# Edge counts of a graph layer built for 10 destinations a step in place of 25

## The reference

```python
def _sage_layer(h, edge_src, edge_dst, deg_inv, W_self, W_neigh, b):
    msg = h[edge_src]
    agg = jax.ops.segment_sum(msg, edge_dst, num_segments=h.shape[0])
    mean = agg * deg_inv[:, None]
    return h @ W_self + mean @ W_neigh + b
...
deg_inv = 1.0 / jnp.maximum(deg, 1.0)
h = jax.nn.relu(_sage_layer(x, edge_src, edge_dst, deg_inv, W_self0, W_neigh0, b0))
out = _sage_layer(h, edge_src, edge_dst, deg_inv, W_self1, W_neigh1, b1)
...
x = x + gnn(layernorm(x), src, dst)     # 1250 nodes, width 1024, 40000 edges sorted by dst
x = x + ffn(layernorm(x))               # router, top 2 of 8 experts
```

## Time and profile before

| | us |
|---|---|
| median of 3 runs | 1111.09 |
| the 3 runs | 1113.34, 1111.09, 1102.71 |
| span of the profiled execution, first to last instruction | 1107.6 |
| busy PE, DVE, ACT, POOL in it | 1068.1, 618.0, 427.1, 193.4 |
| tiles 1 to 7 with the counts | about 63.3 to 309 |

### The profile page before, as it was taken

The page is one execution under the profiler, slowest core; times in us unless marked ns, Lnnn a source line. Parts: engine busy times, 40 slices in busy tenths (PEclk is TensorE's granted clock), DMA queues, the critical chain, the costliest instruction groups (busy, mean ns, idle before and its releaser), DMA issues.

```text
span 1107.6 us, 18245 instructions
## 1 busy us (share of the span) xinstructions
PE 1068.1 (96%) x6565; PEld 1015.3 (92%) x6565; DVE 618.0 (56%) x1090; ACT 427.1 (39%) x934; POOL 193.4 (17%) x192
## 2 busy tenths in 40 slices
PE   5999999999999999999999999999999989999995
PEld 4999999999999999999999999999999679999994
DVE  6678888888752344334323523273222467878883
ACT  5555434453311222121121112164322257777672
POOL 5500000000000002000200020002442124555532
PEclk9999999999999999999999999999999979999998
DMA  6332133213227560004201430276565187999971
GB/s 191 95 105 71 44 108 108 70 43 105 71 71 242 148 186 16 1 19 150 67 1 54 129 76 1 58 244 189 158 186 190 38 302 233 318 304 291 304 220 29
DMA packets 72794, 144.97 MB, mean 131 GB/s; under 512 B 12822, under 2 KB 51667, under 8 KB 68209
## 3 DMA queue, kind: packets, MB, share of 16 engines
q1 hardware_dynamic: 61041, 112.50, 31.7%
q0 software_dynamic: 10976, 30.74, 10.7%
q10 hardware_dynamic: 672, 0.32, 0.1%
HBM read 108.40 MB, written 42.96 MB: 137 GB/s over the span
## 4 chain that ended last, share of the span: by engine, by line
PE 91%; DVE 3%; issue 2%; DMA 1%; DVEq 1%; ACT 1%; POOLq 0%; SPq 0%; POOL 0%; ACTq 0%
PE ps L1482 20%; PE ps L976 14%; PE ps L1554 10%; PE ps L2132 9%; PE ps L1521 9%; PE ps L1211 8%; PE ps L2153 6%; PE ps L821 4%; PE ps L735 3%; PE ps L2118 2%; PE ps L716 1%; DVE key_hot L814 1%; PE ps L921 1%; PE ps L1540 1%; DVE adj L828 1%
## 5 line engine op out<-in xcount | busy, mean ns | idle before, releaser
L1444 POOL TENSOR_TENSOR s_rows<-s_rows,b1t 125x1368 f32<-125x1368 f32 (+3 forms) x9 | 23.7, 2655 | 572.1 <-DMA s_rows<-in_x 572.1
L828 DVE TENSOR_TENSOR adj<-ps,adj 125x250 f32 x212 | 87.7, 414 | 42.0 <-PE ps L821 33.7
L976 PE MATMUL ps<-h_lo,w_hi 128*128 128x418 f32 x336 | 108.6, 372 | 0.0
L976 PE MATMUL ps<-h_hi,w_hi 128*128 128x418 f32 x336 | 100.3, 379 | 0.0
L1521 PE MATMUL ps<-z_hi,adj 125*125 125x342 f32 (+1 forms) x300 | 95.0, 322 | 1.4 <-DVE s_rows L1753 1.4
L1521 PE MATMUL ps<-z_lo,adj 125*125 125x342 f32 (+1 forms) x300 | 94.3, 319 | 0.0
L976 PE MATMUL ps<-h_hi,w_lo 128*128 128x418 f32 x336 | 93.4, 359 | 0.0
L2226 DVE TENSOR_TENSOR w_lo<-w_raw,w_hi 128x2048 fp32r<-128x2048 f32 x34 | 77.8, 2288 | 25.6 <-ACT w_hi L2181 20.8
L1211 PE MATMUL ps<-adj,y_hi 125*128 125x416 f32 (+1 forms) x240 | 85.8, 357 | 2.2 <-DVE layer_out L1276 1.6
L1211 PE MATMUL ps<-adj,y_lo 125*128 125x416 f32 (+1 forms) x240 | 85.4, 356 | 0.0
L821 PE MATMUL ps<-key_hot,src_hot 125*125 125x250 bf16 x424 | 80.8, 271 | 3.4 <-DVE adj L828 3.1
(11 more groups left out here) (301 smaller groups left out, 2685.6 us busy)
## 6 DMA issues: line engine op xcount, KB each, us to landing
w_raw<-in_L_ffn_ew SPq DMA_DIRECT2D x34, 1024.0 KB
xin<-in_x SPq DMA_DIRECT2D x10, 448.0 KB
t_d<-xn SPq DMA_DIRECT2D x10, 448.0 KB
base<-x_d POOLq DMA_DIRECT2D x10, 448.0 KB, 4.2
out<-base POOLq DMA_DIRECT2D x10, 448.0 KB, 3.5
y_d<-y_hi SPq DMA_DIRECT2D x7, 625.0 KB
y_d<-y_lo SPq DMA_DIRECT2D x7, 625.0 KB
self_d<-self SPq DMA_DIRECT2D x7, 625.0 KB
```

The source lines that it names most:

```text
L828: e.tensor_tensor(cols, ps[0:P, 5 + b % 2, 0:KW].rearrange("p (t w) -> p t w", t=NT), cols, ALU.add).then_inc(self.took, 1)
L976: mm = e.matmul(BANK(m, own, c), wt[:, own, k, :], ht[:, k, a:a + w], start=(k == 0 and p == 0), stop=(k == KT - 1 and p == 2))
```

## The change

`W` becomes 10, so a step's moving operand has 100 columns (`KW`) in place of 250. There are 125 windows in place of 50, so `FAST` becomes 288 steps. The sources' one-hot becomes 128 columns wide and all 128 are the stationary operand. The steps are spread evenly over the 106 slots in which counts are made, two or three to a slot, at even distances in the slot's nine matmuls. `SPAN` (the offset between windows in the key) becomes 256. The table of windows is made from one matmul ahead, and the table of columns from a second one after `first_product(e, 1, 1)`, in the same place of bank 2; the banks of tile 0 and of the later tiles are renamed (`TURN_OF`, `DEGREES`) so that bank 2 is the last one taken. TensorE now waits for `s_ecast` 8 ahead of `first_product(e, 1, 2)` in place of 7 ahead of `first_product(e, 0, 2)`.

```diff
-W = 25
+W = 10
-SPAN = 1024
+SPAN = 256
+TURN_OF = (0, 1, 4, 3, 2)
+DEGREES = (3, 2, 5)
-PER = 2
-PW = P + 1
+PW = 128
+SEQ = max(PW, KW)
...
+        S.at = max(S.at, R_WORK + RING * G * PW * 2 + 5 * 4 * NCH)
-        seq_i = S("seq_i", [P, KW], I32)
-        seq16 = S("seq16", [P, KW], F16)
+        seq_i = S("seq_i", [P, SEQ], I32)
+        seq16 = S("seq16", [P, SEQ], F16)
...
             if i == 9:
                 e.wait_ge(s_ecast, 5)
-                for at, t in ((0, past), (256, past_d)):
-                    mm = e.matmul(ps[0:P, 2, at:at + FAST], ones[0:NW, 0:P], t[:], start=True, stop=True)
-                mm.then_inc(s_etp, 1)
+                e.matmul(ps[0:P, 2, 0:FAST], ones[0:NW, 0:P], past[:], start=True, stop=True).then_inc(s_etp, 1)
             if i == NT:
-                e.wait_ge(s_ecast, 6)
+                e.wait_ge(s_ecast, 7)
+                e.matmul(ps[0:1, 2, 0:FAST], ones[0:NW, 0:1], past_d[:], start=True, stop=True)
                 e.matmul(ps[0:1, 2, 496:497], ones[0:P, 0:1], col[:, 8:9], start=True, stop=True).then_inc(s_etp, 1)
...
-            e.wait_ge(s_etp, 7)
+            e.wait_ge(s_etp, 6)
             link(e.tensor_scalar(window[:], ps[0:P, 2, 0:FAST], -float(SPAN), float(SPAN), ALU.mult, ALU.add))
             link(e.tensor_scalar(tabj[:], ps[0:1, 2, 0:FAST], 1.0, None, ALU.subtract))
+            e.sem_inc(s_ecast, 1)
         def chunk_table(e, link):
+            e.wait_ge(s_etp, 7)
             link(e.scalar_tensor_tensor(out=junk[0:1, 0:FAST], in0=step_n[0:1, :], scalar=float(G),
-                                        in1=ps[0:1, 2, 256:256 + FAST], op0=ALU.mult, op1=ALU.add))
+                                        in1=ps[0:1, 2, 0:FAST], op0=ALU.mult, op1=ALU.add))
...
-        BANK = lambda m, own, c: ps[:, (3 * (2 * m + own) + c) % 5, 0:COLS[c][1]]
-        FIRST_BANK = lambda own, c: ps[:, ((0, 1, 2), (3, 0, 4))[own][c], 0:COLS[c][1]]
+        BANK = lambda m, own, c: ps[:, TURN_OF[(3 * (2 * m + own) + c) % 5], 0:COLS[c][1]]
+        FIRST_BANK = lambda own, c: ps[:, ((0, 1, 4), (3, 0, 2))[own][c], 0:COLS[c][1]]
...
-                first_product(e, 1, 1, 0)
+                first_product(e, 1, 1)
                 tables_between(e, NT)
-                first_product(e, 1, 1, 1)
                 e.wait_ge(lo, 2 * NT)
-                e.wait_ge(s_ecast, 7)
                 first_product(e, 0, 2)
...
-                    mm = e.matmul(ps[0:P, 5 + b % 2, 0:KW], src_hot[:, b, g, 0:P], key_hot[:, b, g, :], start=(g == 0), stop=(g == G - 1))
+                    mm = e.matmul(ps[:, 5 + b % 2, 0:KW], src_hot[:, b, g, :], key_hot[:, b, g, :], start=(g == 0), stop=(g == G - 1))
...
-            return [s for s in range((m - 1) * TILE + PER * t, (m - 1) * TILE + PER * t + PER) if s < FAST]
+            i = (m - 1) * SLOTS + t
+            return range(STEPS_TO(i), STEPS_TO(i + 1))
...
             turned(e, 0, 0)
+            e.wait_ge(s_ecast, 8)
             first_product(e, 1, 2)
...
-                        if n in (4, 8):
-                            for s in counted_at(m, t)[n // 8:n // 8 + 1]:
+                        now = counted_at(m, t)
+                        for i, s in enumerate(now):
+                            if n == 9 * (i + 1) // len(now) - 1:
                                 by_order.multiply(e, s, s % RING)
```

More of the change, by code:

```diff
@@ L184, in build @@
         falls = S("falls", [P, NCH], F32)
-        assert S.at <= R_WORK + RING * G * (PW + KW) * 2
+        assert S.at <= R_WORK + RING * G * PW * 2 + 5 * 4 * NCH
         S = Region(R_SLAB + 12288)
@@ L398, in _ @@
             e.memset(d_next[:], 1 << 20).then_inc(s_ones, 1)
-            e.iota(seq_i[:], [[1, KW]], base=0, channel_multiplier=0).then_inc(s_iota, 1)
+            e.iota(seq_i[:], [[1, SEQ]], base=0, channel_multiplier=0).then_inc(s_iota, 1)
             e.iota(step_i[:], [[1, FAST]], base=0, channel_multiplier=0).then_inc(s_iota, 1)
@@ L899, in build @@
         LOWS = {11: 0, 13: 1, 15: 2}
-        TILE = PER * SLOTS
-        REST = FAST - (KT - 2) * TILE
-        assert 0 < REST <= PER * 10
+        TURNS_OF_COUNTS = (KT - 2) * SLOTS + 10
+        STEPS_TO = lambda i: min(i, TURNS_OF_COUNTS) * FAST // TURNS_OF_COUNTS
         def high_group(e, g, out):
@@ L926, in sums @@
                 for k in range(NT):
-                    mm = e.matmul(ps[:, 3 + c, 0:w], ones_, adj_[:, k, a:a + w], start=(k == 0), stop=(k == NT - 1))
+                    mm = e.matmul(ps[:, DEGREES[c], 0:w], ones_, adj_[:, k, a:a + w], start=(k == 0), stop=(k == NT - 1))
                 mm.then_inc(s_deg, 1)
@@ L933, in largest_degree @@
                 e.wait_ge(s_deg, c + 1)
-                e.tensor_reduce(deg_max[:, c:c + 1], ps[0:1, 3 + c, 0:w], AX.X, ALU.max).then_inc(s_big, 1)
+                e.tensor_reduce(deg_max[:, c:c + 1], ps[0:1, DEGREES[c], 0:w], AX.X, ALU.max).then_inc(s_big, 1)
             e.wait_ge(s_big, 3)
@@ L1120, in _ @@
             for c, (a, w) in enumerate(COLS):
-                e.tensor_scalar(yT[:, a:a + w], ps[:, 3 + c, 0:w], 1.0, None, ALU.max).then_inc(s_drow, 1)
+                e.tensor_scalar(yT[:, a:a + w], ps[:, DEGREES[c], 0:w], 1.0, None, ALU.max).then_inc(s_drow, 1)
             for c, (a, w) in enumerate(COLS):
```

## The result

The changed kernel takes 1127.62 us (median of 4, 1126.17 to 1130.34) beside 1110.3 for the kernel before; the ratio is 1.0173, with a 95% interval of 1.014 to 1.0206. It is slower by 1.7%, where the forecast was 0.6% with a range that ended at 1127.0.

The account below looks back on a forecast made before the run. TensorE's chain was taken as the bound, with stops behind VectorE's adds. Terms -1.4 (steps), +7.5 (register loads) and +0.3 (start) gave +6.4 us: 1114.0 against the profiled 1107.6, 1117.5 against the runs' median; range 1100 to 1127.

Parts of the forecast that it names:

- What bounds the kernel: TensorE busy almost throughout, 91% of the last-ending chain; count steps cost 46.6 us, plus stops at VectorE's adds.
- the 7.5 us: Waits of TensorE before count steps in tiles 1 to 7 of the kernel before, taken as stops behind VectorE's adds.
- TensorE's part of a step: Two intervals a step, 0.22 us falling to 0.157; 288 steps cost 45.2 us against 46.6, a gain of 1.4.
- The second interval: From second count matmul to next product matmul: stays at 0.110 us, set by the float32 weight load.
- (c): Rival, chance 0.04: the float32 weight load hides after a bf16 matmul, a step is 2 x 0.047; 1099 us or less.
- (d): Rival, chance 0.04: the 128-column stationary load is slow, both intervals 0.11 us, steps +16.8 us; 1132 us.
- VectorE's part: Shorter adds and key one-hots: two steps cost VectorE 1.25 us in place of 1.89; no more the bound than before.
- The register load: Slow table loads in VectorE's queue delay adds and stop TensorE: 15 us lost where 7.5 are now, +7.5 us.
- (b): Rival, chance 0.21: stops pile up as loads, slab and ScalarE's load add, +16 us; 1126 us.
- ScalarE's part: 76 more steps, about 22 us of activations, cost nothing; lost cover would show as VectorE's one-hots waiting on `key_now`.
- Start: Tables ready near 55.0 us in place of 54.2, the turned tile at 57.7 to 57.9: +0.3 us.
- What would show it: Signs: intervals 0.11 and 0.047 us, 15 or more VectorE register loads over 1.5 us, L821 waits about 15 us.

Follow-up runs that it names:

- x16: Kernel before, VectorE's window register loads taken once and reused: count stretch 234.7 us against 240.1; one execution took 1104.2 us.
- x3: Changed kernel with 125 of the 128 columns of the sources' one-hot as stationary operand: ratio 1.0173 to the kernel before.
- x1: Changed kernel, VectorE loads four window entries once and reuses them for all 288 steps: count stretch 243.2 us against 260.7; its time isn't comparable.
- x17: Changed kernel, VectorE's register loads taken once and the slabs' low parts cut to 8 elements: count stretch 239.2 us against 260.7; time not comparable.
- x9: Changed kernel with the weight slab's low part put ahead of the register load in VectorE's queue: ratio 1.019 to the kernel before.
- x2: Changed kernel, ScalarE loads four chunk entries once and reuses them for all steps: ratio 1.0181 to the kernel before.
- x4: Kernel before with 128 columns in the sources' one-hot, all of them the stationary operand: ratio 1.0029 to the kernel before.
- x6: Kernel before with the low parts of the weight slabs of tiles 1 to 7 moved from VectorE to GpSimd: ratio 1.0113.
- x13: Changed kernel with two table entries in a register load in place of four, on VectorE and ScalarE: ratio 1.055 to the kernel before.

## Why the prediction was wrong, point by point

**What bounds the kernel:** right in kind. TensorE's chain, and its stops at VectorE's adds, in the first half of a tile. The size was misread: the 7.5 us are waits of the weight loads, and a weight load that stands under the running product waits before TensorE does. The weight load at 115.16 us shows 0.75 us and its matmul 0.42. TensorE's idle time in the stretch was 3.4 us, and without VectorE's loads the stretch is 5.4 shorter (x16).

**TensorE's part of a step, -1.4 us forecast, about +3 by the intervals.** The second interval held at 0.112, as the float32 floor said, and the one that the stream sets (from the second count load to the next product load) fell to 0.047. What failed is the count of intervals: the step has a third one. I took the first count load as hidden under the product ahead of it, since it is in the kernel before; the quick load of 128 columns isn't, and adds the 0.015 from the first count load to the second. Nothing in the earlier trace rows shows it, where such loads follow each other only. The step costs 0.169, not 0.157, and the 0.215 of today are less than the 0.22 of the sum. Rivals (c) and (d) are out, the floor stands. The rule of the Trainium skill that I had set beside it ("TensorE: Matmul & The Clock Gate", section "Weight-path perf modes — Fast Weight Load (FWL) and DoubleRow") holds as far as it goes: x3's loads last 0.137 us with 125 columns and the changed kernel's 0.098 with 128.

**VectorE's part:** the sizes were right: the add 0.26 us for 0.41 (forecast 0.16 less), the keys' one-hot 0.36 for 0.67, from odd to even add 0.48 forecast and 0.49 measured (107.23 to 107.72 us in the same timeline), from even to odd 0.77 forecast and 0.78 measured.

**The register load, the term that was mis-sized: +7.5 us forecast, about +17.6 measured** (the stretch's 20.6 less the 3.0 of the steps). Its mechanism was right (x1, x16). A stretch without stops would be 234.6 us long in the kernel before and 237.6 in the changed one (the busy times of x16 and x17). So what the stops cost went from 5.5 to 23.1 us, where the sum has 7.5 and 15. Three things make up the 10 us:

- The start was too high, 7.5 for 5.5, as said above: 2.0.
- The stops themselves came to 19.7 us (16.0 of idle time and the 3.7 that the idle time leaves out) against 15: 4.7. I had taken two slow loads in a tile today and 2.5 after. There are 21 over 0.5 us in the kernel before and 23 in the changed one, about three a tile. And I had taken the slab at 0.3 us since it "often lies over a load". In the kernel before it does; with the uneven steps it comes behind a load in slot 2 of five tiles and beside one in two. One such block is 2.0 + 1.2 us against a reserve of 1.57, and TensorE stands 2 us where my sum had 0.95 + 0.3. That the two add up is seen in tile 2 alone; x9 doesn't show a price for it.
- The granted clock was put at nothing, without a reason: 3.4 us in tiles 2 and 6, behind stops of 2.0 and of 1.0 and 0.8 us.

The case of slab and loads adding up was my rival (b), 0.21 and 1126. The measured 1127.6 is near it, in part by luck: (b) too had the steps 4.4 us too cheap and no lower clock, and what lies behind the stretch was 2.4 us shorter in the profiled execution.

**ScalarE's part:** nothing forecast. Its loads cost TensorE nothing (x2, idle time 15.9 for 16.0 us). Its cover does give way once: the stop of 1.2 us in tile 1 of x1 and x17 comes over `key_now`, the sign that the forecast had named.

**Start:** +0.3 forecast, none measured (the first count load at 63.8 us, 63.9 before). Timeline of the changed kernel, tables, then the turned tile that answers to the earlier trace rows:

```profile
53.05 0.44 DVE L541 SCALAR_TENSOR_TENSOR junk<-step_n,ps 1x288 f32<-1x288 f32 x1 [2.77 <-PE ps L492]
...
54.56 0.23 DVE L548 CAST ones_r<-ones 125x128 fp32r<-125x128 f32 x1
...
57.46 0.55 PEld L923 LDWEIGHTS ps<-ident,yT 128*125 128x125 f32 x4
```

The tables are ready at 54.8, 0.6 later than before, and it delays nothing.

**What would show it:** "15 or more" register loads over 1.5 us was wrong, there were 11, and 12 in the kernel before. The waits of the count steps' weight loads (L821, now L823) were a bad witness in both kernels. In the changed one the idle time of 0.19 us before most count steps is counted there, 61.7 us in all, and is no stop.

**In one sentence:** the sum of +6.4 us failed in its register-load term (+7.5, measured +17.6, with the lower clock left out of it) and in its step term (-1.4, measured +3.0, by a third interval of 0.015 us).

## What to carry to other kernels

Count a reserve between two engines in time, not in steps: two banks of short steps hold less than two of long ones, and here halving the moving work cut the reserve from 2.15 to 1.57 us while the blocks in the consumer's queue stayed as long. Where two such blocks can stand one behind the other, price the sum, and look whether the new step pattern lets them meet. Before a narrower operand is counted as a gain, add up all intervals between weight loads: behind each count step stood a float32 weight load of 0.11 us, and 100 moving columns in place of 250 didn't shorten it. Read TensorE's stops from its own idle time, not from its weight loads'. And before a few us between two profiled executions are put down to an edit, look at the granted clock in the same stretch: here it made up all of the 3.2 us of x2 and 3.4 of the 3.7 of x9.

## What the runs showed of the hardware

- A register load from SBUF in VectorE's queue took 0.34 us for four entries, 0.53 for two and 0.60 for eight, and up to 2.3, 4.0 and 4.0 us in the stretch in which the stores of a tile are in flight. That the transfers make it slow rests on where the slow loads lie; no run moved the stores.
- A stationary load of 128 columns in bf16 lasted 0.098 us and of 125 columns 0.137, but the load of 128 left the port idle for the length of the product ahead (0.19 us), and nothing was won (x3, x4).
- With a float32 operation of 2.4 us on GpSimd beside it, one of VectorE's one-hots lasted until that operation's end: 2.27 us for 0.41 at 85.6 us of x6, and in all 13 cases of its stretch one was longer than 1.2 us.
- TensorE's granted clock fell to 0.50 at 113.2 and at 270.2 us of the changed kernel, after TensorE had stood for 2.0 us, and for 1.0 and 0.8 us. It didn't fall in tiles 1, 3 and 5, where the longest stops were 1.3 to 1.4 us, nor anywhere in the stretch of the kernel before, whose longest was 0.56. In x13, with stops of up to 3.0 us, it fell in every tile.
